# A decoder of four layers on one core: both expert mixtures sort all their tokens in one group

## The chip, the cores and the metric

The kernel runs on one core of a Trainium2 chip. Everything is float32. The time is the device time of one execution in microseconds; the comparison uses the median of several executions. TensorE does the matmuls and the transposes (a matmul with an identity), VectorE (DVE), ScalarE (ACT) and GpSimd (POOL) the elementwise work, SyncE (SP) starts the plain DMAs, and POOL also starts the indirect DMAs that scatter rows.

## The reference, cut to what matters

The activation x has 4 batches of 512 tokens of width 256. Twelve stages run one after the other, four layers of an attention, a cross attention and a feed-forward part:

```python
x = x + _L1_xattn_ref(ctx_1024, _layernorm(x), ...)      # the same form in layers 2 and 3
...
x = x + _L2_ffn_ref(_layernorm(x), router_w, w1, w2)
...
x = x + _L3_ffn_ref(_layernorm(x), Wg, W1, b1, W2, b2, W3, b3)
```

The cross attentions of layers 1 to 3 take their queries from the 512 tokens; keys and values come from the 512 tokens and from 64 rows of a second input, the context:

```python
kv = jnp.concatenate([x, lat], axis=1) @ Wkv
...
attn = jax.nn.softmax(dots, axis=-1)
out = jnp.einsum('bhij,bhjd->bhid', attn, v)
```

In the roles of the kernel, x of this excerpt is the 64-row context and lat the 512 tokens, so each head has 512 + 64 keys. The two feed-forward parts of layers 2 and 3 are mixtures of 8 experts, and each token goes to the two best:

```python
probs = jax.nn.sigmoid(xf @ router_w.T)                  # layer 2
topw, sel = jax.lax.top_k(probs, 2)                      # combine = topw / sum(topw)
h = jnp.square(jax.nn.relu(jnp.einsum('td,edw->tew', xf, W1e)))
out = jnp.einsum('ted,te->td', jnp.einsum('tew,ewd->ted', h, W2e), combine)
...
topv, topi = jax.lax.top_k(xt @ Wg.T, 2)                 # layer 3, weights softmax(topv)
h = jax.nn.silu(jnp.einsum('th,efh->etf', xt, W1) + b1) * (jnp.einsum('th,efh->etf', xt, W2) + b2)
eo = jnp.einsum('etf,ehf->eth', h, W3) + b3
```

## The kernel before

x stays in SBUF (`x_res`) as 16 token tiles of 128 tokens, four to a batch. Each stage is a function with one instruction list for each engine; between stages the engines meet. `sparse_experts` (from L4148) is run twice: turn 0 for layer 2, turn 1 for layer 3. It does not compute all experts for all tokens. It sorts rows by expert through HBM and multiplies only what is needed:

- **Routing.** DVE and ACT normalize the 16 tiles into `rows`, TensorE turns them in pieces of four (`piece_turned`, L4356) and multiplies with the router (`route`, L4367). DVE marks the two best experts of each token (`pick`: MAX8 at L4537, MATCH_REPLACE8 at L4540, the mask at L4543).
- **Places.** `rank` (L4376, L4378) counts with matmuls how many rows go to each expert ahead of each token, `put` (L4559 to L4584) makes from it the row index of each token's two copies, `weigh` (L4594 to L4609) the weights of the final sum.
- **Scatters.** POOL writes each token tile twice, once for each of its two experts, with indirect DMAs to `sorted_rows` in HBM (L4298). For the second copy the row's own number, its last column, is raised by one (L4336).
- **Tiles.** Since each expert's rows are rounded up to full tiles, n token tiles give (256 n + 8 x 127) / 128 sorted tiles, rounded down. The tokens are in two groups, `GROUP_TILES = (4, 12)`: 15 and 31, together 46 sorted tiles. SP loads them in chunks of 3 (`load_sorted`, L4264), after all scatters of their group. For each tile TensorE turns the rows (L4390), ACT copies the expert's up weights to a fixed place (L4494), TensorE multiplies up (L4404: 16 matmul records in turn 0, 32 in turn 1, where a second product is gated), ACT and DVE make the hidden rows, TensorE multiplies down (L4420), DVE copies the result to a ring of four buffers (L4678, in turn 1 with the bias at L4681), and POOL scatters it to its token's place in `expert_outputs` (L4307).
- **The second group inside the tiles.** Its `rank(1)`, `put(1)` and `weigh(1)` stand behind the second tile. Its 24 scatters stand in POOL's list between the output scatters: three, then one output, eight times over.
- **Final sums.** When the outputs are stored, SP fetches them (L4269), and DVE adds them to x with two operations per token tile, weight times row plus x (L4686, L4689). The first batch (4 token tiles) is fetched and added while later tiles run; 12 token tiles, 24 operations, stand at the end of the stage.

Before the first stage that needs them the weights are loaded by SP at the head of the stage: in turn 1 the columns of biases, 8 MB of up weights, 1 MB of bias rows (L4249) and 4 MB of down weights (L4250), all ahead of `load_sorted(0)`.

In the cross attentions of layers 1 to 3 the heads go in pairs, 8 pairs for each of four batches in layers 1 and 2, 4 in layer 3, 80 in all. For each pair `attended` (L2441, L2444) multiplies the values with the turned probabilities: for four key blocks of 128 and both heads (head h writes half h of the rows of a PSUM bank), then for the context block of 64 keys, where both weights and data of head h are on partitions 64h to 64h+63. The scores of the next pair (L2491) and the transposes of the probabilities (L2411) stand around it.

## Time and profile before

| | us |
|---|---|
| median of 3 executions | 3911.28 (3911.06 to 3914.19) |
| the profiled execution | 3942.55 |
| its span, first to last instruction | 3940.4 |
| l0 and l1_attn (0 to 605.65) | 605.65 |
| l1_xattn | 735.33 |
| l1_ffn and l2_attn | 608.82 |
| l2_xattn | 787.40 |
| l2_ffn, mixture, turn 0 (2737.2 to 2999.9) | 262.70 |
| l3_attn | 149.50 |
| l3_xattn | 444.10 |
| l3_ffn, mixture, turn 1 (3593.5 to 3940.4) | 346.90 |

TensorE is busy for 3495.3 us of the span (89%), VectorE for 2191.8 (56%), ScalarE for 1495.8 (38%) and GpSimd for 1370.0 (35%). In the l1_xattn stage TensorE is busy 701.45 of 735.33 us, in turn 0 of the mixture 212.15 of 262.70, in turn 1 285.71 of 346.90. The mean granted TensorE clock is 0.93 of full speed over the run, 0.85 over turn 0 and 0.89 over turn 1. A row of the timeline is one instruction or several of one kind in a row: its start, its length, the engine, the line, what it writes and reads, and in brackets how long the engine was idle before it and what released it.

### The profile page before, as it was taken

How to read it: one execution, taken by the hardware profiler on the slowest of the kernel's cores; microseconds unless marked ns; L12 is line 12 of the kernel's file. 1: busy time of each engine (PE TensorE's matmuls, PEld its weight loads, DVE VectorE, ACT ScalarE, POOL GpSimd, SP SyncE). 2: the span in 40 equal slices, each digit the busy share in tenths (PEclk: the TensorE clock that was granted, in tenths of full speed). 3: DMA queues.
4: the chain of work that ended last, by engine and by line, in shares of the span. 5: the costliest groups of instructions: out<-in, count | busy, mean ns of one | idle time of the engine just before them, and what ended most of it. 6: DMA issues, size and time to landing. Idle time of an engine off the chain costs nothing. (4 is left out here: it accounts for less than half of the span.)

```text
span 3940.4 us, 54458 instructions
## 1 busy us (share of the span) xinstructions
PE 3495.3 (89%) x18930; PEld 2240.6 (57%) x18930; DVE 2191.8 (56%) x5367; ACT 1495.8 (38%) x3040; POOL 1370.0 (35%) x1904
## 2 busy tenths in 40 slices
PE   7998897899999977888798999998896989995997
PEld 5675684445555566344444555555794445554896
DVE  5374444645556468666367676765234466664454
ACT  3253112433434364233244444443352144442453
POOL 2141441423323255232254444533422144442311
PEclk9999978999999988899799999999798889996998
DMA  2004001000000000000100000001221000003212
GB/s 100 1 1 123 14 1 46 1 1 1 1 1 1 13 1 24 1 1 1 49 1 1 1 1 1 1 1 76 99 80 57 4 25 1 1 1 160 71 60 84
DMA packets 48718, 108.85 MB, mean 28 GB/s; under 512 B 6660, under 2 KB 32900, under 8 KB 46404
## 3 DMA queue, kind: packets, MB, share of 16 engines
q1 hardware_dynamic: 40964, 84.88, 6.3%
q0 software_dynamic: 7488, 20.49, 1.5%
q8 instruction: 158, 2.59, 0.3%
q14 instruction: 108, 0.88, 0.1%
HBM read 70.67 MB, written 34.68 MB: 27 GB/s over the span
## 5 line engine op out<-in xcount | busy, mean ns | idle before, releaser
L2653 POOL TENSOR_SCALAR probs<-probs,inv_sum 128x512 f32<-128x512 f32 x640 | 437.7, 697 | 1008.3 <-DVE inv_sum L2774 1008.1
L2616 ACT ACTIVATE probs<-psum_banks,neg_max 128x576 f32<-128x576 f32 x640 | 468.5, 737 | 742.5 <-DVE neg_max L2857 742.5
L2857 DVE TENSOR_REDUCE neg_max<-psum_banks 128x1 f32<-128x576 f32 x640 | 455.0, 752 | 213.4 <-PE psum_banks L2491 206.8
L2491 PE MATMUL psum_banks<-keys_T,queries_T 64*128 64x288 f32 x2560 | 406.0, 436 | 52.5 <-ACT probs L2616 43.2
L2783 DVE COPY probs_T<-psum_banks 128x512 f32<-128x512 f32 x640 | 409.2, 681 | 4.5 <-PE psum_banks L2411 4.5
L2491 PEld LDWEIGHTS psum_banks<-keys_T,queries_T 64*128 64x128 f32 x2560 | 224.5, 189 | 269.2 <-ACT probs L2616 147.9
L2411 PE MATMUL psum_banks<-ident,probs 128*128 128x128 f32 x2560 | 356.5, 283 | 3.2 <-POOL probs L2653 2.3
L2411 PEld LDWEIGHTS psum_banks<-ident,probs 128*128 128x128 f32 x2560 | 280.3, 143 | 128.2 <-POOL probs L2653 63.3
L2441 PE MATMUL psum_banks<-probs_T,values 128*64 128x512 f32 x1280 | 310.9, 607 | 2.2 <-issue 2.2
L4404 PE MATMUL psum_banks<-sorted_T,tile_weights 128*128 128x128 f32 x2208 | 270.1, 279 | 9.2 <-ACT tile_weights L4494 4.9
L4404 PEld LDWEIGHTS psum_banks<-sorted_T,tile_weights 128*128 128x128 f32 x2208 | 262.2, 196 | 10.7 <-issue 10.6
L2853 DVE TENSOR_TENSOR psum_banks<-psum_banks,key_mask 128x128 f32<-128x128 f32 x192 | 57.5, 299 | 280.1 <-PE psum_banks L2491 280.1
L4420 PE MATMUL psum_banks<-w_L_experts_down,hidden_T 128*128 x736 | 183.3, 394 | 19.4 <-DVE expert_rows L4678 8.7
L4307 POOL DMA_INDIRECT expert_outputs<-expert_rows,output_index x92 | 90.3, 982 | 297.4 <-DVE expert_rows L4681 126.7
L2665 POOL TENSOR_TENSOR square_sum<-square_sum,neg_half 128x8 f32<-128x8 f32 x102 | 167.1, 1639 | 70.8 <-DVE square_sum L2749 69.3
L4420 PEld LDWEIGHTS psum_banks<-w_L_experts_down,hidden_T 128*128 128x128 f32 x736 | 137.4, 197 | 37.7 <-issue 21.7
L2346 PE MATMUL psum_banks<-w_L_xattn_Wkv,batch_normed_T 128*128 128x512 f32 x320 | 158.7, 620 | 0.0
L2441 PEld LDWEIGHTS psum_banks<-probs_T,values 128*64 128x64 f32 x1280 | 78.8, 136 | 133.8 <-issue 124.1
L4494 ACT COPY tile_weights<-w_L_experts_up 128x1024 f32 (+1 forms) x92 | 135.3, 1472 | 23.5 <-issue 23.5
L1962 ACT ACTIVATE probs_T<-psum_banks 128x512 f32<-128x512 f32 (+3 forms) x128 | 83.0, 701 | 127.7 <-PE psum_banks L1899 126.9
L2656 POOL TENSOR_TENSOR context_probs<-probs,inv_sum 128x128 f32<-128x128 f32 x320 | 128.9, 403 | 0.0
L2616 ACT ACTIVATION_READ_ACCUMULATOR probs<-psum_banks,neg_max 128x1 f32 x640 | 125.4, 196 | 0.0
(535 smaller groups left out, 6119.2 us busy)
## 6 DMA issues: line engine op xcount, KB each, us to landing
normed<-sorted_rows SPq DMA_DIRECT2D x30, 385.5 KB
sorted_rows<-zero_rows SPq DMA_DIRECT2D x8, 1028.0 KB, 14.5
w_L_experts_down<-in_L_experts_down SPq DMA_DIRECT2D x2, 4096.0 KB, 37.1
normed<-expert_outputs SPq DMA_DIRECT2D x8, 1024.0 KB, 7.9
w_L_xattn_Wkv<-in_L_xattn_Wkv SPq DMA_DIRECT2D x2, 2048.0 KB, 8.5
w_L_experts_up<-in_L_experts_up SPq DMA_DIRECT2D x1, 4096.0 KB, 13.0
sorted_rows<-zero_rows SPq DMA_DIRECT2D x4, 899.5 KB, 14.1
x_res<-in_x SPq DMA_DIRECT2D x4, 512.0 KB, 6.9
```

The source lines that it names most:

```text
L2346: last = pe.matmul(k.ps[:, 7, :], rows, wkv[:, c, W + a * 512:W + (a + 1) * 512], start=c == 0, stop=c == KC - 1)
L2411: last = pe.transpose(k.ps[:, 4 + n % 2, c * P:(c + 1) * P], prob[:, (b * NS + s) % PB, at + c * P:at + (c + 1) * P], k.ident[:, :])
L2441: last = pe.matmul(k.ps[r, 6, :], values[:, b % VB, c, (2 * j + h) * 64:(2 * j + h + 1) * 64], pT[:, q % 2, h, c, :], start=c == 0, stop=F ...
L2491: last = pe.matmul(k.ps[:, 2 * h + a, 0:HALF], qT[r, b % 2, j, t * P:(t + 1) * P], kT[r, j, k0:k0 + HALF], start=True, stop=True)
L2616: act.activation(prob[:, g % PB, h * w:(h + 1) * w].rearrange("p (a n) -> p a n", a=2), k.ps[:, 2 * h:2 * h + 2, 0:HALF], ACT.Exp, bias=nm ...
L2653: pool.tensor_scalar(w, w, inv[:, g % 4, h:h + 1], 1.0, ALU.mult, ALU.mult).then_inc(shared, 1)
L2665: pool.tensor_tensor(ss[:, i % 4, 2, :], ss[:, i % 4, 1, :], k.half[:, 0:8], ALU.pow).then_inc(inverted, 1)
L2783: dve.tensor_copy(pT[:, q % 2, h, :, t * P:(t + 1) * P], k.ps[:, 4 + n % 2, :].rearrange("p (c q) -> p c q", q=P)).then_inc(copied, 1)
L2857: dve.tensor_reduce(nmax[:, g % 4, h:h + 1], k.ps[:, 2 * h:2 * h + 2, 0:HALF], AX.XY, ALU.max, negate=True).then_inc(maxed, 1)
L4404: last = pe.matmul(ps[:, 2 * (n % 2) + part, f * P:(f + 1) * P], wt[:, n % 2, c, part * 512 + f * P:part * 512 + (f + 1) * P], xsT[:, n % ...
L4420: last = pe.matmul(ps[:, 6, 0:D], h[:, n % 2, f * P:(f + 1) * P], w_down[:, f // F, f % F * D:f % F * D + (E - 1) * STEP + D][:, bass.ds(a ...
L4494: act.copy(wt[:, n % 2, :, :], w_up[:, :, 0:(E - 1) * STEP + UP][:, :, bass.ds(at, UP)]).then_inc(weights_copied, 1)
```

## The change

- Each turn has its own groups, `MIXTURES = ((16,), (16,))`: one group of all 16 token tiles, which gives 39 sorted tiles. Routing, rank, places and weights are made once, for all tokens; all 32 scatters stand in POOL's list ahead of the first output scatter, and the first load of sorted rows waits for all of them. The ring of results has six buffers.
- ACT copies the up weights of the first two tiles before it moves the first turned rows.
- Final sums: all four batches are fetched at the end. For each token tile DVE adds the first row times its weight, ACT multiplies the second row by its weight in place, and POOL adds it to x.
- In turn 1 the bias rows and the down weights are loaded after the first two chunks of sorted rows; the columns of biases have a semaphore of their own.
- The context values of a pair get a block per head of 128 rows, in which the other head's 64 rows are zero (written once per stage by two DVE memsets); the context product then contracts over 128 rows.

```diff
-GROUP_TILES = (4, 12)
-GROUP_FIRST = (0, 4)
-GROUP_SORTED = tuple((2 * n * P + E * (P - 1)) // P for n in GROUP_TILES)
+MIXTURES = ((16,), (16,))
+HEAD = 4
...
-OUTPUT_RING = 4
+OUTPUT_RING = 6
...
-                sp.dma_start(w_down[:, :, :], w_down.src[:, :, :]).then_inc(down_loaded, 16)
+                if bias is None:
+                    load_late_weights()
...
                 load_sorted(0)
                 load_sorted(1)
+                if bias is not None:
+                    load_late_weights()
...
-                sp.wait_ge(combined, TT)
-                for b in range(1, B):
-                    fetch(b, TT * (b - 1))
+                for b in range(EARLY // TT, B):
+                    fetch(b, TT * b - EARLY)
...
+                if GROUPS == 1:
+                    pool.wait_ge(normed, NT)
+                    pool.wait_ge(indexed, 2)
+                    for t in range(NT):
+                        scatter(t, rows[:, t, :], 0, scattered_0)
+                    pool.wait_ge(copied_again, HEAD)
+                    for t in range(HEAD):
+                        scatter(t, again[:, t, :], 1, scattered_again)
+                    pool.wait_ge(scattered_0, first_scattered)
+                    late = rows[:, HEAD:NT, D:D + 1]
+                    pool.tensor_scalar(late, late, 1.0, 1.0, ALU.add, ALU.mult).then_inc(next_ids, 1)
+                    pool.wait_ge(next_ids, 1)
+                    for t in range(HEAD, NT):
+                        scatter(t, rows[:, t, :], 1, scattered_again)
...
                 for n in range(done, NTILES):
                     scatter_rows(n)
+                for t in range(EARLY, NT):
+                    pool.wait_ge(halfway, t + 1)
+                    pool.wait_ge(second_scaled, t - EARLY + 1)
+                    pool.tensor_tensor(k.x[:, t, :], k.x[:, t, :], got[:, t - EARLY, 1, :], ALU.add).then_inc(combined, 1)
...
+                for t in range(EARLY, NT):
+                    act.wait_ge(fetched[t // TT], 16)
+                    act.mul(got[:, t - EARLY, 1, :], got[:, t - EARLY, 1, :], gate[:, 1, t:t + 1]).then_inc(second_scaled, 1)
...
+                if GROUPS == 1:
+                    copy_weights(0)
+                    copy_weights(1)
 
                 move_rows(0)
                 move_rows(1)
-                copy_weights(0)
-                copy_weights(1)
...
-                                last = pe.matmul(k.ps[r, 6, :], vc[r, j, :], pTc[r, q % 2, :], start=False, stop=True)
+                                last = pe.matmul(k.ps[r, 6, :], vc[:, h, j, :], pTc[:, q % 2, :], start=False, stop=True)
```

POOL's list in turn 0, from the first scatter to the end of the stage, before. `sorted_rows_0` and `_1` are the two groups' sorted rows, `expert_outputs` the results:

```order
L4298 DMA sorted_rows_0<-normed,row_index 1920x257 x8
L4298 DMA sorted_rows_1<-normed,row_index 3968x257 x3
L4307 DMA expert_outputs<-expert_rows,output_index 9985x256
L4298 DMA sorted_rows_1<-normed,row_index 3968x257 x3
L4307 DMA expert_outputs<-expert_rows,output_index 9985x256
L4298 DMA sorted_rows_1<-normed,row_index 3968x257 x3
L4307 DMA expert_outputs<-expert_rows,output_index 9985x256
L4298 DMA sorted_rows_1<-normed,row_index 3968x257 x3
L4307 DMA expert_outputs<-expert_rows,output_index 9985x256
L4336 TENSOR_SCALAR normed<-normed 128x12
```

The same place after, to the end of the stage:

```order
L4324 DMA sorted_rows_0<-normed,row_index 4992x257 x20
L4355 TENSOR_SCALAR normed<-normed 128x12
L4324 DMA sorted_rows_0<-normed,row_index 4992x257 x12
L4333 DMA expert_outputs<-expert_rows,output_index 9089x256 x39
L4388 TENSOR_TENSOR x_res<-x_res,normed 128x256 x16
```

The 24 scatters that stood between output scatters now stand ahead of all of them, and 16 additions stand behind the last.

TensorE's list at the head of turn 0, before (pieces turned, routed, the first tiles, and the second group's rank behind them; the rank's matmuls shrink by 8 columns each, down to 128x8):

```order
L4367 MATMUL psum_banks<-w_L_ffn_router_w,normed 128x8 x16
L4390 MATMUL psum_banks<-ident,normed 128x128 x4
L4404 MATMUL psum_banks<-sorted_T,tile_weights 128x128 x8
L4390 MATMUL psum_banks<-ident,normed 128x128 x2
L4404 MATMUL psum_banks<-sorted_T,tile_weights 128x128 x8
L4376 MATMUL psum_banks<-gate_mask,w_before_token 128x104
L4378 MATMUL psum_banks<-gate_mask,ones 128x96
```

The same place after (here too the rank's matmuls shrink down to 128x8, and the tiles follow):

```order
L4411 MATMUL psum_banks<-w_L_ffn_router_w,normed 128x8 x16
L4420 MATMUL psum_banks<-gate_mask,w_before_token 128x136
L4422 MATMUL psum_banks<-gate_mask,ones 128x128
L4422 MATMUL psum_banks<-gate_mask,ones 128x120
```

The rank has moved from behind the second tile's product to ahead of the first turned tile, and covers 16 token tiles instead of 12.

SP's list at the head of turn 1, before:

```order
L4246 DMA w_L_bias_columns<-in_L_bias_columns 128x64
L4247 DMA w_L_experts_up<-in_L_experts_up 128x16384
L4249 DMA row_vectors<-in_rows 128x2048
L4250 DMA w_L_experts_down<-in_L_experts_down 128x8192
L4264 DMA normed<-sorted_rows_0 128x3x257 x5
```

And after:

```order
L4264 DMA w_L_bias_columns<-in_L_bias_columns 128x64
L4265 DMA w_L_experts_up<-in_L_experts_up 128x16384
L4287 DMA normed<-sorted_rows_0 128x3x257 x2
L4269 DMA row_vectors<-in_rows 128x2048
L4270 DMA w_L_experts_down<-in_L_experts_down 128x8192
```

Bias rows and down weights now stand behind the first two chunks of sorted rows.

## Rows read from the trace of the kernel before

**Rows 1.** TensorE's timeline, one pair in l1_xattn: start, length, then the instruction

```profile
773.46 1.03 PE L2441 MATMUL psum_banks<-probs_T,values 128*64 128x512 f32 x4
...
773.89 0.60 PE L2441 MATMUL psum_banks<-probs_T,values 128*64 128x512 f32 x2
...
774.42 1.08 PE L2444 MATMUL psum_banks<-context_probs_T,context_values 64*64 64x512 f32 x4
775.43 1.24 PE L2491 MATMUL psum_banks<-keys_T,queries_T 64*128 64x288 f32 x8
...
779.12 0.51 PE L2491 MATMUL psum_banks<-keys_T,queries_T 64*128 64x288 f32 x2 [1.42 <-ACT probs L2616]
```

**Rows 2.** Tile stretches: length, busy of PE, PEld, DVE, ACT, POOL, PEclk, DMA share, GB/s

```profile
2774.98:2971.72 196.74, 183.15 (x1186) 168.58 (x1187) 61.22 (x150) 89.14 (x134) 66.74 (x68) 0.93 0.24 78
3643.26:3906.11 262.85, 254.86 (x1906) 242.22 (x1907) 123.64 (x242) 130.94 (x135) 66.39 (x68) 0.99 0.18 59
```

**Rows 3.** Timeline of turn 0, last scatters, first tiles, second group's rank

```profile
2764.98 0.97 POOL L4298 DMA_INDIRECT sorted_rows<-normed,row_index  x1 [0.30 <-issue]
...
2767.80 11.75 SPq L4264 DMA_DIRECT2D normed<-sorted_rows  x3
...
2769.41 0.99 DVE L4537 MAX8 gate_top<-gate_row 128x8 f32<-128x14 f32 x12 [12.43 <-ACT gate_row L4473]
...
2771.04 0.66 PE L4390 MATMUL psum_banks<-ident,normed 128*128 128x128 f32 x2 [2.03 <-DMA normed<-sorted_rows]
...
2772.16 0.69 PE L4390 MATMUL psum_banks<-ident,normed 128*128 128x128 f32 x2 [0.46 <-ACT sorted_T L4482]
2772.26 0.21 DVE L4543 TENSOR_SCALAR gate_mask<-gate_marked 128x96 f32<-128x96 f32 x1
...
2774.98 3.75 PE L4404 MATMUL psum_banks<-sorted_T,tile_weights 128*128 128x128 f32 x16 [2.13 <-ACT tile_weights L4494]
...
2778.95 2.36 PE L4404 MATMUL psum_banks<-sorted_T,tile_weights 128*128 128x128 f32 x16
...
2781.35 2.76 PE L4378 MATMUL psum_banks<-gate_mask,ones 128*128 128x96 f32 x24
...
2787.64 0.97 POOL L4298 DMA_INDIRECT sorted_rows<-normed,row_index  x1 [21.69 <-DVE row_index L4574]
```

**Rows 4.** Timeline of turn 0, last tiles and final sums

```profile
2964.47 1.95 PE L4404 MATMUL psum_banks<-sorted_T,tile_weights 128*128 128x128 f32 x16
...
2968.21 1.95 PE L4404 MATMUL psum_banks<-sorted_T,tile_weights 128*128 128x128 f32 x16
...
2981.89 1.46 SPq L4269 DMA_DIRECT2D normed<-expert_outputs  x3
2987.44 0.48 DVE L4686 SCALAR_TENSOR_TENSOR x_res<-normed,gate_weights,x_res 128x256 f32<-128x256 f32 x1 [8.85 <-DMA normed<-expert_outputs]
...
2998.05 0.48 DVE L4689 SCALAR_TENSOR_TENSOR x_res<-normed,gate_weights,x_res 128x256 f32<-128x256 f32 x1
```

**Rows 5.** DVE and POOL beside each other in l3_attn (timeline)

```profile
3003.43 0.38 DVE L4064 TENSOR_SCALAR normed<-x_res,token_mv,token_rstd 128x256 f32<-128x256 f32 x1
...
3016.39 2.49 POOL L4039 TENSOR_TENSOR x_res<-x_res,row_vectors 128x512 f32<-128x512 f32 x2
...
3017.84 1.20 DVE L4064 TENSOR_SCALAR normed<-x_res,token_mv,token_rstd 128x256 f32<-128x256 f32 x1 [7.07 <-PE psum_banks L3913]
```

**Rows 6.** POOL's groups by form: an addition of 128x256 (busy, mean ns)

```profile
L2672 POOL TENSOR_TENSOR x_res<-x_res,row_vectors 128x256 f32<-128x256 f32 x32 | 22.3, 732 | 0.0
```

**Rows 7.** Timeline of turn 1, mask, first tile, two late tiles

```profile
3628.62 0.21 DVE L4543 TENSOR_SCALAR gate_mask<-gate_marked 128x96 f32<-128x96 f32 x1
...
3643.26 5.49 PE L4404 MATMUL psum_banks<-sorted_T,tile_weights 128*128 128x128 f32 x32 [2.76 <-ACT tile_weights L4494]
...
3889.77 3.74 PE L4404 MATMUL psum_banks<-sorted_T,tile_weights 128*128 128x128 f32 x32
3895.29 3.74 PE L4404 MATMUL psum_banks<-sorted_T,tile_weights 128*128 128x128 f32 x32
```

**Rows 8.** DMA issues of the page: count, KB each, us to landing

```profile
w_L_experts_up<-in_L_experts_up SPq DMA_DIRECT2D x1, 4096.0 KB, 13.0
```

220 lines of the change are left out of this document (127 added, 93 removed).

## The prediction

> **What bounds the kernel now.** I read the stages first, then the tile stretches of the two mixtures, then their two ends row by row. The reader is to see three things. In the mixtures the tiles bound, but not all of the time: turn 0 takes 196.74 us from the first tile's up product to the last one's, while two late tiles in a row start 3.73 us apart (2964.47, 2968.21), so 45 steps would be 167.9; 28.9 us are lost, TensorE is busy for only 183.15, and its clock is 0.93 [rows 2, 4]. Turn 1 takes 262.85 for 45 steps of 5.52 (3889.77 to 3895.29), 248.4; 14.4 are lost [rows 2, 7]. The loss stands where POOL's list holds three sorting scatters for each output scatter: 4 x 1.27 = 5.1 us of POOL (0.97 each and 0.30 of issue [rows 3]) against 3.73 for a tile, and four result buffers are soon full. Second, the head of each stage is a chain (mask, rank, places, scatters, load) in which TensorE mostly waits. Third, the cross attentions run on TensorE with little idle time; what the context product costs there counts 80 times.
>
> **Context product, 80 pairs.** It now has the form of its neighbours (contraction over 128 rows). The last two double steps of L2441: the one at 773.46 is followed by the next at 773.89, .43 for two records in one form; the last two before the form changes take 773.89 to 774.42, .53. The four context records take 774.42 to 775.43, 1.01; four of L2441, 773.46 to 774.42, take .96 although the form changes at their end [rows 1]. In one form, I expect .10 less at the change and .05 less in the product: 0.15 x 80 = **-12.0**. No row shows the new form in this place, so bounds: -8 (only the change, .10) to -13, and 0 as a rival. The next pair's scores find TensorE at once at 775.43, and the wait of 1.42 us at 779.12 is for ACT's probabilities, which follow from scores that also come earlier, so the saving carries on. The two memsets lie in DVE's wait for the context and cost nothing; if that cover were gone they would cost their own length once in a stage.
>
> The Trainium skill ("TensorEngine Tiling (Array Packing)", Theoretical Speedup) gives a product with a contraction of at most 64 rows up to twice the speed of the full array; by it a 128-row form would double the four records, +1.0 x 80 = +80. The rows speak against it: the 128-row records already run at .43 for two heads' halves, not slower than the 64-row ones at about .5. I give it no chance of its own beyond the rivals.
>
> **Turn 0, the head.** In the before case the mask of 12 token tiles ends at 2772.47. MAX8 to the mask took 2.85 for 12 tiles, so four more cost .95, and the fourth piece's routing in front of it some .3 (an estimate): 2773.7. The rank: 24 records took 2.76, .115 each; 16 token tiles need 34: 3.9 at the full clock. After an idle time TensorE runs at half (3.75 at 2774.98 for what later took 1.95 [rows 3, 4]), which gives 7.8. The clock comes back on the way; I take the middle, 6.0: 2779.8. From the rank's end (2784.11) to POOL's first scatter (2787.64) 3.53 passed; with 16 tiles 3.7: 2783.6. The 32 scatters go at 1.28, the ids raised in between cost about 1.0: the last starts 31 x 1.28 + 1.0 = 40.7 later, 2824.3. From the last scatter to the load 2.82 (2764.98 to 2767.80), to the first turned tile 3.24 (2771.04), to the up product 1.8: the second turning ends 1.12 + .69 behind the first's start, and the weights, which were copied late before (2.13 us of waiting at 2774.98), are there already. So the first up product starts at 2832.1, **+57.1** [rows 3].
>
> **Turn 0, the tiles.** No scatter stands between the outputs any more: POOL needs 1.27 a tile, six buffers. I take 3.73 throughout, and .6 for the first two tiles at a half clock (3.97 from 2774.98 to 2778.95, and part of the next) [rows 3, 4]. 39 tiles are 38 steps: 2832.1 + 141.7 + .6 = 2974.4 against 2971.72: **+2.7**. In terms: +57.1 head, -28.9 lost time, -26.1 for seven tiles, +.6. Bounds: the rank -2.1 to +1.8.
>
> **The final sums, each turn.** Before, the fetch is issued at 2981.89, DVE starts 5.55 later and ends at 2998.53: 16.64, of it 11.1 for 24 operations. Now 16 token tiles need .48 of DVE and .73 of POOL each [rows 4, 6], ACT's multiplication beside them. If DVE and POOL did not disturb each other, POOL would set the pace: 5.55 + .5 (the first DVE operation) + 16 x .75 = 18.0, +1.4. If one fully blocks the other, 1.21 each: 5.55 + 19.3 = 24.8, +8.2. The trace has such a meeting: POOL's two additions run 3016.39 to 3018.88, a DVE operation that alone takes .38 starts at 3017.84 and takes 1.20, to 3019.04 [rows 5]; had it waited for POOL's whole end it would have ended at 3019.26, so .22 overlapped. I take .48 + .73 - .22 = 1.0: 5.55 + .5 + 16.0 = 22.05, **+5.4** in each turn, +10.8 together.
>
> The Trainium skill ("SBUF — State Buffer", SBUF: two separate sides) says that a DVE operation with two SBUF inputs and a GpSimd operation that reads SBUF hold the shared port pair as an exclusive lock and the loser fully blocks. The trace agrees nearly. That is the upper bound, and a rival below.
>
> **Turn 1.** The mask ends at 3628.83. With the same +1.2 for 16 tiles and the same 58.4 from there to the up product (2773.7 to 2832.1), the first tile starts at 3688.5, +45.2 [rows 7]. 38 steps of 5.52 and .1: 3898.4 against 3906.11: -7.7. Then the late weights: the load is issued 5.0 before the first tile, 3683.5; 5 MB follow behind it. 4 MB took 13.0 to land [rows 8], so 5 MB take some 16.2, and they land at about 3700.5. The first down product is wanted behind the second up product: 3688.5 + 5.5 (half clock) + 3.9 = 3697.9. About 3 us of stall, and 1 for the clock that falls in it: +4.0 (bounds 0 to +6). Turn 1: **-3.7**. The waits added are `down_loaded` on TensorE, behind which only this tile's products stand, and `bias_loaded` on DVE at the first result, whose bias rows are issued before the down weights.
>
> **The sum.** -12.0 + 2.7 + 5.4 - 3.7 + 5.4 = -2.2. The profiled execution's span goes from 3940.4 to 3938.2, with the 2.15 around it 3940.4 instead of 3942.55. The profiled run stands 31.3 above the median; I take the difference as the same for both: 3911.28 - 2.2 = **3909.1**. Shorter loads of small arrays, ten instead of twelve fills and one sigmoid or exp less lie beside other work and count nothing.
>
> **Rivals.**
> - *The engines do not block each other in the sums.* For: the DVE result of tile t+1 does not touch what POOL adds for tile t, so the starts can interleave. Against: rows 5. Tails +1.4 each, sum -10.2: 3901.1; if the down weights are there in time too, -14.2: 3897.1.
> - *Full blocking*, as the page's rule would have it, 1.21 for each tile: tails +8.2 each, sum +3.4: 3914.7. For: rows 5, where .96 of 1.20 was a wait.
> - *Slower: the context product saves nothing*, since the .53 and 1.01 are not the form but the turn to other data, or since ACT's chain (softmax) bounds the pair. The point from which it decides is a pair whose scores wait for ACT, as at 779.12. Against: TensorE is 95% busy in that stage. Sum +9.8: 3921.1.
> - *Slower: the lost time in the tiles is not POOL's list*, but the loading of sorted rows beside the output scatters; then it stays with one group. Against: late in the turn, with loads and output scatters alike, steps are 3.73. +28.9 and +14.4 less half of what only the second group's start can explain (about 5): 3909.1 + 38 = 3947.
> - *The change does not do what it says*: the seven tiles less are fixed by the list, so no.
>
> **How the numbers follow.** Chances: forecast .48, no blocking .20, full blocking .14, nothing saved in the context .13, lost time stays .05. 0.2% is 7.8 us, about what a measurement tells from no change. Faster by more: .20, and .14 of the forecast's own spread (rank in time, context at -13, weights in time): .34. Slower by more: .13 + .05 and .05 of the spreads: .23. Within: .43. The range takes in all cases but the last: 3896 to 3922; the likeliest case's own is 3903 to 3915.
>
> **What would show it.** The context records: the four take .86 instead of 1.01, and the record before them follows at .43. The first up product of turn 0 lies about 95 us behind the stage's start instead of 37.8 (2774.98 - 2737.2), and steps are 3.73 from the third tile on. In the final sums POOL's additions start 1.0 apart (.7: the first rival; 1.2: the second). In turn 1 TensorE waits about 3 us for the DMA of the down weights ahead of the first down product. What would make it wrong: a step between tiles that isn't 3.73 and 5.52; scatters at a pace other than 1.28 when 32 stand in a row; a clock that comes back later than after the rank.

## The result and the profile after

The changed kernel takes 3957.47 us (median of four executions, 3955.79 to 3958.22), the kernel before in the same comparison 3912.74 (3911.06 to 3918.84): a ratio of 1.0108, with a 95% interval from 1.0096 to 1.012, 44.7 us slower. Three of the four executions of the kernel before are the ones of the table of before. The prediction was 3909.1 with a range that ended at 3922. It was wrong in sign and in size. One execution of the kernel before among the experiments (e12), of 12353.8 us at a granted clock of 0.45, is left out of its median.

A second number stands beside it from the start. The two traces differ by 13.7 us only (spans 3940.4 and 3954.1). The traced execution of the kernel before had taken 31 us more than its own median, that of the changed kernel takes what all its executions take. Where these 31 us belong is the larger part of what follows.

The stages of the changed kernel, from each stage's first load to the next one's: l1_xattn, l2_xattn, turn 0 of the mixture, l3_xattn, turn 1. The columns are those of [rows 2] (length, busy PE, PEld, DVE, ACT, POOL, clock, DMA share, GB/s):

```profile
608.87:1339.59 730.72, 696.66 (x3560) 389.28 (x3560) 395.32 (x762) 286.26 (x673) 228.18 (x395) 0.98 0.02 7
1949.64:2732.22 782.58, 737.40 (x3816) 414.71 (x3816) 509.83 (x1060) 346.26 (x774) 350.47 (x478) 0.97 0.02 7
2732.22:3009.35 277.13, 176.77 (x1144) 165.23 (x1144) 78.05 (x237) 98.26 (x159) 86.80 (x92) 0.77 0.28 99
3159.24:3599.30 440.06, 382.88 (x1928) 214.01 (x1928) 286.80 (x638) 178.34 (x394) 189.04 (x260) 0.95 0.02 7
3599.30:3954.10 354.80, 248.12 (x1768) 235.95 (x1768) 132.95 (x319) 133.06 (x159) 86.74 (x92) 0.81 0.27 98
```

Against the table of before: the cross attentions are 4.6, 4.8 and 4.0 us shorter, turn 0 is 14.4 longer, turn 1 7.9 longer. TensorE is busy for 177 of 277 us in turn 0, where it was busy for 212 of 263, and its mean clock there fell from 0.85 to 0.77: it has less to do and waits longer ahead of it. The first stage, whose code is the same, took 608.87 instead of 605.65.

The head of turn 0 after the change, against [rows 3]: the mask, the rank, the first and the last of 32 scatters, the first turned tile, and three up products:

```profile
2770.09 0.23 DVE L4598 TENSOR_SCALAR gate_mask<-gate_marked 128x128 f32<-128x128 f32 x1
...
2771.05 6.84 PE L4422 MATMUL psum_banks<-gate_mask,ones 128*128 128x128 f32 x32
...
2781.86 1.25 POOL L4324 DMA_INDIRECT sorted_rows<-normed,row_index  x1 [38.32 <-DVE row_index L4629]
...
2822.53 0.97 POOL L4324 DMA_INDIRECT sorted_rows<-normed,row_index  x1 [0.30 <-issue]
...
2828.75 0.66 PE L4434 MATMUL psum_banks<-ident,normed 128*128 128x128 f32 x2 [50.86 <-DMA normed<-sorted_rows]
...
2830.35 3.62 PE L4448 MATMUL psum_banks<-sorted_T,tile_weights 128*128 128x128 f32 x16
...
2834.19 1.95 PE L4448 MATMUL psum_banks<-sorted_T,tile_weights 128*128 128x128 f32 x16
...
2837.93 1.95 PE L4448 MATMUL psum_banks<-sorted_T,tile_weights 128*128 128x128 f32 x16
```

TensorE stands still for 50.86 us between the rank and the first turned tile. From there each tile follows the one ahead at 3.73 without a gap, which the tile stretches of both turns show, first to last up product:

```profile
2830.35:2972.14 141.79, 141.79 (x980) 132.38 (x980) 44.38 (x98) 75.30 (x113) 34.97 (x36) 0.99 0.21 65
3697.62:3913.76 216.14, 211.33 (x1587) 201.31 (x1587) 96.93 (x174) 109.62 (x114) 34.98 (x36) 0.98 0.19 65
```

In turn 0 TensorE is busy for all of 141.79 us. In turn 1 4.8 us are idle, in one place, the wait for the down weights that the prediction has:

```profile
3697.62 5.43 PE L4448 MATMUL psum_banks<-sorted_T,tile_weights 128*128 128x128 f32 x32
...
3703.10 3.74 PE L4448 MATMUL psum_banks<-sorted_T,tile_weights 128*128 128x128 f32 x32
3711.66 3.54 PE L4464 MATMUL psum_banks<-w_L_experts_down,hidden_T 128*128 x8 [4.81 <-DMA w_L_experts_down<-in_L_experts_down]
```

And the end of turn 0, against [rows 4]: the fetch, the first operations of DVE and POOL (16 of each in a row), and the next stage's first operation on DVE:

```profile
2982.43 2.28 SPq L4292 DMA_DIRECT2D normed<-expert_outputs  x4
...
2987.97 12.99 DVE L4749 SCALAR_TENSOR_TENSOR x_res<-normed,gate_weights,x_res 128x256 f32<-128x256 f32 x16 [8.92 <-DMA normed<-expert_outputs]
2988.63 13.60 POOL L4388 TENSOR_TENSOR x_res<-x_res,normed 128x256 f32<-128x256 f32 x16 [7.77 <-ACT normed L4567]
...
3009.40 1.47 DVE L4057 BATCH_NORM_STATS2 token_stat<-x_res 128x6 f32<-128x256 f32 x4 [8.43 <-PEq L45]
```

The additions run at 0.85 us a token tile and end at 3002.23, 19.80 us behind the fetch. Then 7.2 us pass in which no engine computes. Before, the next stage began 1.5 us behind DVE's last operation (2998.53 in [rows 4] to 2999.99).

### The profile page after: what moved, and what is told of

Its sections match the earlier page's. It is cut to its first block and busy times, and to the rows that moved or that the text cites. A ratio compares the mean times of both kernels' runs of the same rounds, so it can differ in the third digit from the quotient of the medians.

```text
span 3954.1 us, 53033 instructions
## 1 busy us (share of the span) xinstructions
PE 3414.8 (86%) x18450; PEld 2187.3 (55%) x18450; DVE 2155.6 (55%) x5225; ACT 1475.0 (37%) x3028; POOL 1379.2 (35%) x1922
## 5 line engine op out<-in xcount | busy, mean ns | idle before, releaser
L4448 PE MATMUL psum_banks<-sorted_T,tile_weights 128*128 128x128 f32 x1872 | 225.1, 278 | 0.0
L4448 PEld LDWEIGHTS psum_banks<-sorted_T,tile_weights 128*128 128x128 f32 x1872 | 218.9, 195 | 0.1
L4333 POOL DMA_INDIRECT expert_outputs<-expert_rows,output_index x78 | 75.8, 972 | 317.0 <-DVE expert_rows L4744 142.7
L4464 PE MATMUL psum_banks<-w_L_experts_down,hidden_T 128*128 x624 | 149.4, 383 | 7.0 <-DMA w_L_experts_down<-in_L_experts_down 4.8
L4532 ACT COPY tile_weights<-w_L_experts_up 128x1024 f32 (+1 forms) x78 | 114.6, 1472 | 46.6 <-DVE weight_offsets L4639 28.1
L4464 PEld LDWEIGHTS psum_banks<-w_L_experts_down,hidden_T 128*128 128x128 f32 x624 | 113.7, 192 | 20.5 <-issue 8.0
```

The lines of the kernel that those rows point to most:

```text
L4448: last = pe.matmul(ps[:, 2 * (n % 2) + part, f * P:(f + 1) * P], wt[:, n % 2, c, part * 512 + f * P:part * 512 + (f + 1) * P], xsT[:, n % ...
L4464: last = pe.matmul(ps[:, 6, 0:D], h[:, n % 2, f * P:(f + 1) * P], w_down[:, f // F, f % F * D:f % F * D + (E - 1) * STEP + D][:, bass.ds(a ...
```

## The experiments

All ratios are to the kernel before, run beside it on the same chip. There were six sessions, each on another chip: on four of them the kernel before takes 3941 to 3944 us, on two 3912. The executions of a session agree in this. No chip was used in two sessions, so chip and session can't be told apart; "kind of chip" below means no more than that. On which chips the comparison above and the first trace were taken is not known.

| kernel | before there | this, us | ratio (95% interval) |
|---|---|---|---|
| e0 before | 3942.7 | 3941.3 | 1.0000 (0.9986 to 1.0014) |
| e1 before + context product | 3942.7 | 3932.3 | 0.9974 (0.9965 to 0.9984) |
| e2 change, two groups in both turns | 3942.7 | 3922.5 | 0.9946 (0.9929 to 0.9963) |
| e3 change, sums on DVE | 3942.7 | 3944.3 | 1.0009 (0.9999 to 1.0019) |
| e4 change | 3941.8 | 3955.6 | 1.0035 (1.0024 to 1.0045) |
| e5 change, early weights | 3941.8 | 3948.5 | 1.0011 (1.0001 to 1.0020) |
| e6 change, one group in turn 0 only | 3941.8 | 3935.6 | 0.9981 (0.9971 to 0.9991) |
| e7 change, one group in turn 1 only | 3941.8 | 3936.7 | 0.9986 (0.9974 to 0.9997) |
| e8 two groups, sums on DVE | 3943.9 | 3907.8 | 0.9907 (0.9892 to 0.9922) |
| e9 one group, sums on DVE, early weights | 3943.9 | 3937.9 | 0.9985 (0.9976 to 0.9994) |
| e10 change, last six tiles' sums on DVE | 3943.9 | 3944.5 | 1.0003 (0.9994 to 1.0012) |
| e11 as e8, four result buffers | 3912.5 | 3885.1 | 0.9932 (0.9919 to 0.9946) |
| e12 before / e13 change | 3941.4 | 3937.4 / 3954.9 | 0.9991 / 1.0036 (1.0021 to 1.0051) |
| e14 before / e15 change | 3911.7 | 3915.8 / 3952.0 | one execution each |

### Is it 44.7 us or 13.9: the two kernels run again

No edit in any of these.

> The kernel before, unchanged. Its profiled execution took 3942.55 us, 31 more than the median of its plain ones (3911.28), while the changed kernel's profiled and plain executions agree (3955.79 against 3957.47). Theory A: the kernel before has two ways to run, and the trace that was read is of the longer one; a fresh trace is then near 3912 and shows which stretch is 31 us shorter, by my reading the lost time in the tile stretches (28.9 us in turn 0, 14.4 in turn 1). Theory B: the profiler itself costs it 31 us, and the fresh trace is at 3942 again with plain executions at 3912. Theory C: the difference lies in other stages, and the tile stretches lose 28.9 and 14.4 us in both.

> The changed kernel, unchanged, once more beside the kernel before on the same chip. The comparison on record gave a ratio of 1.0108 (44.7 us), but the two traces differ by 13.7 us of span only, and on the chip of the first experiments the kernel before takes 3942.7 us instead of 3912.7. Theory A: the 31 us are the chip's or the session's, not the change's, and side by side the ratio is what the traces say: 13.7 us, 1.0035 (3956 where before is 3943). Theory B: the changed kernel costs 45 us wherever it runs; then 3988 where before is 3943. Theory C: the changed kernel is at 3950 to 3957 on every chip, and only the kernel before moves between 3912 and 3943; the ratio then depends on the chip, 1.002 to 1.011.

The kernel before took 3941.3 there, so theory B of the first, that the profiler costs the 31 us, falls: plain and traced executions agree on that chip. The changed kernel took 3955.6 beside 3941.8, 13.9 us or 0.35% more, as the two traces had said (13.7). But 3955.6 is also within 2 us of what it had taken in the comparison on record (3957.5), where the kernel before was at 3912.7. Only one of the two kernels moves with the chip, theory C of the second. To see where, a trace of the kernel before on the faster kind of chip was needed.

> The kernel before, once more. On three chips it took 3942 to 3944 us, on a fourth 3912.5, as in its first executions. The kernel with two groups, DVE sums and four buffers, traced on that fourth chip, had a tile stretch of turn 0 (first to last up product) of 175.6 us, against 192.8 for its sister with six buffers traced on another. Theory: if this execution falls on a chip where the time is 3912, its tile stretches take some 178 and 253 us instead of 193 to 198 and 263; where it is 3942, they are as before. Rival: the stretches are the same in both, and the 31 us lie in other stages.

> The changed kernel once more, on the same chip as the run above. Theory: its tile stretches run at 3.73 and 5.52 us a tile whatever the chip, so it takes 3954 to 3958 on every chip; the ratio is 1.0035 where the kernel before takes 3942 and 1.011 where it takes 3912. Rival: it moves with the chip as the kernel before does, and the ratio stays 1.0035.

This pair fell on a chip of the slower kind and repeated the numbers: 3937.4 and 3954.9. The next pair fell on the faster kind.

> The kernel before, a third time, in search of a chip where it takes 3912 us. Theory: on such a chip its two tile stretches take some 178 and 253 us instead of 193 to 198 and 263, all other stages as before. Rival: the stretches are the same, and the 31 us lie in other stages. On a chip where it takes 3942 the run tells only that the stretches are at 193 to 198 and 263 again.

> The changed kernel beside it: 3950 to 3958 on either kind of chip by the theory, 3925 on the faster kind by the rival.

The kernel before took 3915.8 (and 3911.7 in the execution beside it), the changed one 3952.0, one execution each. The tile stretches of the kernel before on this chip, first to last up product of each turn, and turn 0 and turn 1 as a whole, the counterparts of [rows 2]:

```profile
2779.80:2955.61 175.81, 173.15 (x1186) 161.37 (x1187) 61.35 (x150) 89.39 (x134) 65.86 (x68) 0.98 0.27 87
3623.89:3879.75 255.86, 253.63 (x1910) 241.91 (x1910) 124.06 (x242) 131.01 (x135) 68.14 (x68) 0.99 0.19 60
...
2742.15:2983.60 241.45, 202.12 (x1328) 187.12 (x1328) 91.66 (x302) 105.12 (x165) 80.53 (x83) 0.88 0.35 121
3573.40:3913.50 340.10, 286.02 (x2064) 270.92 (x2064) 156.75 (x402) 146.33 (x165) 82.66 (x83) 0.88 0.30 108
```

The stretches take 175.81 and 255.86 instead of 196.74 and 262.85: 20.9 and 7.0 us less, together 27.9, where the two spans (3940.4 and 3913.5) differ by 26.9; the other stages differ by 5 us at most, up and down. With 45 steps of 3.73 and 5.52, only 7.9 and 7.5 us are lost there. So the time that the change was to win back, 28.9 and 14.4 us in [rows 2], is mostly not there on this kind of chip. In turn 0 all of the 7.9 stand in the first three steps from tile to tile (4.0, 7.1 and 8.1 us, up product to up product, instead of 3.73), where the second group's rank runs on TensorE and DVE works out its places; the trace of [rows 3] has the same three (4.0, 7.0 and 8.6). What differs between the chips comes behind them.

What the lost time looks like where it is lost. The kernel before in its first trace, TensorE's timeline:

```profile
2821.02 1.95 PE L4404 MATMUL psum_banks<-sorted_T,tile_weights 128*128 128x128 f32 x16
2828.36 3.78 PE L4420 MATMUL psum_banks<-w_L_experts_down,hidden_T 128*128 x8 [5.38 <-issue]
2831.93 0.63 PE L4390 MATMUL psum_banks<-ident,normed 128*128 128x128 f32 x2
2832.35 3.67 PE L4404 MATMUL psum_banks<-sorted_T,tile_weights 128*128 128x128 f32 x16
2837.52 3.51 PE L4420 MATMUL psum_banks<-w_L_experts_down,hidden_T 128*128 x8 [1.50 <-DVE expert_rows L4678]
```

The same list on the faster kind of chip, at the same place of the program, with the same 24 scatters and 8 outputs in POOL's list and the same four buffers:

```profile
2802.73 1.95 PE L4404 MATMUL psum_banks<-sorted_T,tile_weights 128*128 128x128 f32 x16
...
2806.47 1.95 PE L4404 MATMUL psum_banks<-sorted_T,tile_weights 128*128 128x128 f32 x16
...
2810.20 1.95 PE L4404 MATMUL psum_banks<-sorted_T,tile_weights 128*128 128x128 f32 x16
...
2813.93 1.95 PE L4404 MATMUL psum_banks<-sorted_T,tile_weights 128*128 128x128 f32 x16
```

Steps of 3.73 while POOL scatters at 1.28. No result waits for a buffer in either of the two traces: DVE's copies into the ring (`expert_rows`) never wait for a stored output. And the waits of the first trace in its first 75 us of tiles (engine, what waited, for what: us, times, longest) name releasers that are no program step:

```profile
ACT hidden_T L4509 <- remote: 11.5, 2, 6.7
...
DVE hidden_T L4650 <- issue: 10.1, 2, 7.1
...
PE psum_banks L4420 <- issue: 5.4, 1, 5.4
```

With "remote" and "issue" the profile names no instruction of the program that ended the wait. In the same stretch on the faster chip no operation of DVE and no matmul waits for either. Over the whole traces, waits of this kind of 3 us or more on TensorE, ACT or DVE are in no trace from the faster kind (e11, e14, e15) and in no trace of the changed kernel (after, e4, e13, e15). In the traces of two groups from the slower kind there are 2 to 14, up to 10.9 us long, all but at most one of each trace where the second group's scatters run between tiles; that one, 3.7 to 3.9 us of ACT in turn 0, lies beside the first group's scatters. e6 has them in turn 1 only and e7 in turn 0 only, each in its turn of two groups. What holds the engines there on some chips no view of the trace names. That stays open.

### The context product alone

```diff
-                                last = pe.matmul(k.ps[r, 6, :], vc[r, j, :], pTc[r, q % 2, :], start=False, stop=True)
+                                last = pe.matmul(k.ps[r, 6, :], vc[:, h, j, :], pTc[:, q % 2, :], start=False, stop=True)
```

(e1: with the two-block `vc` and its memsets, on the kernel before)

> The kernel before with the context product of the changed kernel alone. The trace after shows the three cross attention stages shorter by 4.6, 4.8 and 4.0 us, 13.4 together, and the stages ahead of them longer by 3.2. Theory: -13 us against the kernel before, 3899 in plain executions (ratio 0.9966). Rival: what the context product gives is eaten in the stages ahead, since the 3.2 us belong to it: -10. A second rival: the plain executions differ from the profiled ones in these stages and nothing is gained.

It gave 10.5 us, between theory and rival, and the interval (0.9965 to 0.9984, 6 to 14 us) decides for neither. The traces are sharper. The eight value records and the ones behind them, before, with [rows 1], and after:

```profile
772.55 1.94 PE L2441 MATMUL psum_banks<-probs_T,values 128*64 128x512 f32 x8
...
775.08 1.94 PE L2443 MATMUL psum_banks<-probs_T,values 128*64 128x512 f32 x8
776.84 1.03 PE L2446 MATMUL psum_banks<-context_probs_T,context_values 128*64 128x512 f32 x4
777.80 1.24 PE L2493 MATMUL psum_banks<-keys_T,queries_T 64*128 64x288 f32 x8
```

The four context records take 0.96 (776.84 to 777.80) where they took 1.01, and follow the start of the eight value records after 1.76 (1.77 as the median) where it was 1.87 (772.55 to 774.42). That is 0.05 in the product and 0.10 at the change of form, in the median of the pairs of every stage, 0.15 x 80 = 12 us. The three stages are together shorter by 12 to 17 us in all traces with this form, against the first trace of the kernel before, and by 8 to 12 against e14.

### One group or two

```diff
-MIXTURES = ((16,), (16,))
+MIXTURES = ((4, 12), (4, 12))      # e2; ((16,), (4, 12)) in e6, ((4, 12), (16,)) in e7
```

> The changed kernel with the two groups of 4 and 12 token tiles in both turns again; the final sums on three engines for the last 12 token tiles, six result buffers, the late weights of turn 1 and the context product stay. If the one group is what costs the 44.7 us, this one is at the time before less the context product: 3900 to 3908, the three-engine sums and late weights adding 3 to 8 us. If the late weights and sums cost most of it, it stays near 3940. By the profiled stages alone (turn 0 +14.4, turn 1 +7.9) the whole mixture part would be only 22 us, and two groups would be at 3935.

> The changed kernel with one group in turn 0 and two groups (4 and 12 token tiles) in turn 1. Turn 0 took 277.1 us with one group (trace after) and 262.7 with two (the kernel with two groups in both turns). Theory: 14 us slower than the kernel with two groups in both turns (3922.5), 3937. Rival: what one group costs sits in turn 1, and this kernel is at 3925.

> The changed kernel with two groups in turn 0 and one group in turn 1. Turn 1 took 354.8 us with one group (trace after) and 338.6 with two groups and the same late weights. Theory: 16 us slower than the kernel with two groups in both turns, 3938.5, and the two single-group turns add up to the changed kernel, 3952. Rival: the sum is not the parts, since the first turn's length moves the second's clock: more than 5 us off.

With two groups the changed kernel would have been 20 us faster than before on the slower kind of chip. Its two groups are not quite those of before: the second group's rank stands behind the first tile, not the second. One group in turn 0 costs 13 us of that, in turn 1 14, both 33 (ratios 0.9946, 0.9981, 0.9986, 1.0035, over two chips of the slower kind). e2's own expectation had reckoned 22 us for both; the stages of its trace are 14.4 and 16.2 us shorter than those of the changed kernel. That the two costs add up to 27 and not 33 is the rival of e7, but the intervals (4 us and more to either side of each) do not separate 27 from 33. All this is where two groups still lose 25 us in the tiles of turn 0; no kernel with one group in one turn was run on the faster kind.

### The final sums

```diff
                 for t in range(EARLY, NT):
-                    pool.wait_ge(halfway, t + 1)
-                    pool.wait_ge(second_scaled, t - EARLY + 1)
-                    pool.tensor_tensor(k.x[:, t, :], k.x[:, t, :], got[:, t - EARLY, 1, :], ALU.add).then_inc(combined, 1)
...
-                    if t >= EARLY:
-                        return
```

(e3: ACT's loop removed as well, so that DVE makes both operations of each token tile)

> The changed kernel with the final sums on DVE alone (32 operations at 0.46 us, 14.8 us, behind the fetch of all four batches), nothing on ACT and POOL. In the trace after, 7.1 us pass from POOL's last addition (3002.23) to the next stage's start (3009.35), 1.4 us passed from DVE's last before. Theory: the 5.7 us are POOL's own way out of the stage, which was hidden while POOL had been idle for 20 us; then this kernel has a gap of 1.4 and turn 0 is 5 us shorter, turn 1 0.5 longer: 3953 in all. Rival: the gap belongs to the new stage layout and stays: 3958.

3944.3 against 3955.6 for the change, on two chips of the slower kind: 11 us less (ratios 1.0009 and 1.0035) with all 32 operations on one engine, where the theory had some 5. In its trace turn 0 is 5.1 us shorter than in the changed kernel's, as expected, and turn 1 2.2 shorter, not 0.5 longer. The gap is gone (DVE's last operation, the next stage's first):

```profile
2994.98 0.48 DVE L4745 SCALAR_TENSOR_TENSOR x_res<-normed,gate_weights,x_res 128x256 f32<-128x256 f32 x1
...
2996.99 0.76 DVE L4057 BATCH_NORM_STATS2 token_stat<-x_res 128x6 f32<-128x256 f32 x2 [1.53 <-PEq L45]
```

To see whether the gap is POOL's, the last six token tiles were given to DVE:

```diff
-                for t in range(EARLY, NT):
+                for t in range(EARLY, NT - 6):
                     pool.wait_ge(halfway, t + 1)
...
+                    if t == NT - 6:
+                        dve.wait_ge(combined, NT - 6)
```

> The changed kernel with the last 6 of 16 token tiles summed on DVE alone (two operations each), the first 10 on three engines; GpSimd is done some 5 us before the stage ends. Theory A: the 7.1 us from the last addition to the next stage in turn 0 are GpSimd's branch out of the stage and its four clears of semaphores, run after its last addition; then the gap falls to about 1.5 us, and the tail from fetch to next stage from 26.9 to 5.5 + 10 x 0.85 + 12 x 0.46 + 1.5 = 21.5. Theory B: the gap comes with ACT or with the new stage layout; it stays at 7 us. In time: A is 8 us faster than the changed kernel (3948, ratio 1.0015), B the same or 1 us slower.

```profile
2994.04 8.60 POOL L4388 TENSOR_TENSOR x_res<-x_res,normed 128x256 f32<-128x256 f32 x10 [7.80 <-ACT normed L4567]
...
3007.26 0.48 DVE L4756 SCALAR_TENSOR_TENSOR x_res<-normed,gate_weights,x_res 128x256 f32<-128x256 f32 x1
...
3009.81 1.41 DVE L4057 BATCH_NORM_STATS2 token_stat<-x_res 128x6 f32<-128x256 f32 x4 [2.06 <-PEq L45]
```

POOL ends at 3002.64, DVE at 3007.74, and the next stage starts at 3009.81: 7.17 us behind POOL and 2.07 behind DVE. In the changed kernel it was 7.17 behind POOL too (3002.23 to 3009.40). With DVE alone it is 1.5 behind DVE, so in e10 the stage still waits for POOL, by half a microsecond. The gap is POOL's, as theory A says, but not for the clears of semaphores that the theory names. POOL's sequencer has a DRAIN at the end of the stage; here are the kernel before and the changed one (count, the shortest, median and longest of the two turns in ns, the first and the last start):

```profile
L4227 POOLq DRAIN  x2: 7627/7631/7635, 2979.2 to 3917.0; - x2
...
L4244 POOLq DRAIN  x2: 7092/7097/7102, 3001.0 to 3945.7; - x2
```

In the changed kernel it runs from 3001.01 to 3008.11, 5.88 us past the last addition; the clears and the meeting of the engines take the other 1.3, and they are in the 1.5 us of before too. In the kernel before the DRAIN was over at 2986.84, while DVE was still at its sums. Its length is nearly the same with a scatter as POOL's last work (e3, 7.07) as with an addition (7.10); what sets it no run shows. In time e10 is 11 us faster than e4 by the medians of two chips (ratios 1.0003 and 1.0035, some 5 us of uncertainty), and 7.3 by the two turns of the traces; 8 was forecast.

### The late weights

```diff
-                if bias is None:
-                    load_late_weights()
+                load_late_weights()
...
-                if bias is not None:
-                    load_late_weights()
```

> The changed kernel with bias rows and down weights of turn 1 loaded at the head of the stage again, as before the change. In the trace after, TensorE waits 4.8 us for the down weights at 3706.8 and its first down product takes 3.54 at the halved clock instead of 1.89: 6.5 us. Theory: this kernel is 6.5 us faster than the changed one beside it. Rival: the 5 MB at the head slow the stores of sorted rows, and half of it is lost: 0 to 3 us.

7.1 us less, and turn 1 is 6.5 shorter in the trace. The second up product and the first down product of turn 1 follow one another at the full clock:

```profile
3699.56 3.74 PE L4445 MATMUL psum_banks<-sorted_T,tile_weights 128*128 128x128 f32 x32
3703.13 1.89 PE L4461 MATMUL psum_banks<-w_L_experts_down,hidden_T 128*128 x8
```

### What is left of the one group, and a version that is faster

e9 joins the edits of e3 and e5. e8 is e3 with two groups in both turns; its late weights stay. The second group's rank stands behind the first tile here too.

> The changed kernel with both repairs: final sums on DVE alone and bias rows and down weights loaded at the head of turn 1. Alone they gave 11.3 us and 7.1 us. What is left of the change is the one group and the context product. Theory: the two add up, 3955.6 - 18.4 = 3937, ratio 0.9988, so that the one group alone costs some 6 us against two groups in the form of before (3932.3 with the context product). Rival: they overlap (the shorter tail moves nothing when the clock falls again), 3944, ratio 1.0005.

> Two groups in both turns, the context product, six result buffers and late weights of turn 1 kept, the final sums on DVE alone (24 operations for the last 12 token tiles). With two groups and the three-engine sums the time was 3922.5 (0.9946 of before); its stages took 23.8 us from the fetch to the next stage in turn 0 and 24.2 to the end in turn 1, against 18.0 and 20.7 before. Theory: the two sums give back 5.8 + 3.5 us: 3913, ratio 0.9923. Rival: with late weights and more result buffers the DVE sums meet the fetch of the last batch and give nothing: 3922.

The repairs add up: 3937.9, as worked out. The one group, repaired and with the gain of the context product in it, is 6 us faster than before on the slower kind of chip. On the faster kind it was not run; from e9's 17.7 us under e4 and the 44.7 of the comparison it would be some 27 us slower than before, an estimate. The two-group version is 36 us faster than before on the slower kind, 5 us better than its theory. In turn 1 the late weights, which cost 7 us with one group, gain time with two: the last of the first eight scatters is issued 27.5 us behind the stage's start in both kernels, but the first chunks of sorted rows are issued 31.5 us behind it instead of 41.9, where the 5 MB stood ahead of them and the down weights landed at 41.2. The first up product starts 37.7 us behind the stage's start instead of 49.8. No run has two groups with early weights on the changed kernel, so this is read from the traces:

```profile
3606.17 0.91 SPq L4287 DMA_DIRECT2D normed<-sorted_rows  x2
3607.13 0.48 SPq L4269 DMA_DIRECT2D row_vectors<-in_rows  x1
```

The whole turn takes 331.80 instead of 346.9 (the columns of [rows 2] again):

```profile
3574.70:3906.50 331.80, 283.63 (x2064) 266.99 (x2064) 156.40 (x402) 145.90 (x165) 81.28 (x83) 0.91 0.31 111
```

Against e8, e11 changes the ring of results alone, `OUTPUT_RING = 4`:

> The two-group kernel with DVE sums (3907.8, ratio 0.9907) with four result buffers instead of six, nothing else. From the first to the last up product of turn 0 it took 192.8 us for 45 steps of 3.73 (167.9), so 25 us are lost with six buffers too; the kernel before loses 28.9. Theory: the buffers are not what stalls, since POOL's list of 24 scatters among 8 outputs runs at its own 1.28 us and two more buffers only shift the wait: same time within 3 us, ratio 0.9907 to 0.9915. Rival: the buffers give 3 to 6 us in each turn, and this kernel is at 3914 to 3920 (0.9925 to 0.994).

It fell on a chip of the faster kind (before at 3912.5), where it is 27 us faster than before. So its ratio, 0.9932, says nothing of the buffers against 0.9907. Its own trace does. In it the tiles run at 3.73 from the second on, and then DVE waits for stored outputs, four times in a row, of which these are the first three:

```profile
2809.81 0.42 DVE L4732 COPY expert_rows<-psum_banks 128x256 f32<-128x256 f32 x1 [1.19 <-DMA expert_outputs<-expert_rows,output_index]
...
2814.91 0.42 DVE L4732 COPY expert_rows<-psum_banks 128x256 f32<-128x256 f32 x1 [2.55 <-DMA expert_outputs<-expert_rows,output_index]
...
2819.99 0.42 DVE L4732 COPY expert_rows<-psum_banks 128x256 f32<-128x256 f32 x1 [3.83 <-DMA expert_outputs<-expert_rows,output_index]
```

They are 5.1 us apart, the pace of POOL's list, and three steps of TensorE take 4.84, 5.08 and 5.74 us instead of 3.73: 4.5 us more, of which 0.4 are a wait for sorted rows and the rest is lost to a ring of four, as the rival said of this turn and the theory did not. In turn 1 nothing waits for a stored output. Six buffers on this kind of chip were not run. The trace, in which turn 0 took 239.4 us, was also the first sign that the rest of the lost time goes with the chip.

## Why the prediction was wrong, point by point

**The context product: right.** -12.0 predicted, -13.4 in the trace after, -10.5 timed alone. The mechanism (one form, no change) and the size hold, 0.10 and 0.05 us a pair. The sign that the prediction gives for it, .86 for the four context records, is not what its own working says (1.01 less .05), and they took 0.96.

**The head of turn 0: right in kind, 3 us short.** The first up product was to start 94.9 us behind the stage's start and started at 98.1. The scores were ready 1.6 later than taken, and the rank took 7.42 (2770.47 to 2777.89), nearly the upper bound of 7.8, not the middle of 6.0: TensorE ran at half its clock (granted 0.50) through all 34 records. Scatters (1.28), load and turning came as in [rows 3].

**The lost time: the step that failed.** The sum took -28.9 and, inside turn 1's -7.7, -14.4 from [rows 2], times of one traced execution, and set them against a median 31.3 us lower with the sentence that the difference is the same for both kernels. It was not: the 31 us and the lost time are largely the same microseconds. In the one trace of the kernel before from a chip where it takes 3912 (e14) only 7.9 and 7.5 us are lost. Put into the sum of the prediction, this makes +27.9, and -2.2 becomes +25.7.

The mechanism was wrong as well. The prediction says that POOL's list (5.1 us for an output against 3.73 for a tile) fills four buffers. Its own rows leave the ring just short of full: eight outputs at 5.1 us are 41 us, in which TensorE makes 11 tiles, three more than are stored, and the ring holds four. In the kernel before no result waits for a buffer on either kind of chip, and e14 has the same list, four buffers and steps of 3.73. The mechanism exists, but is small: in e11, where the results are further ahead of their scatters from the start, it costs some 4 us. Of the 28.9 us of turn 0 some 8 belong to the first three steps, with the second group's rank, on both kinds of chip, and the rest to pauses whose cause is open. The rival that the lost time is not POOL's list was given .05; it expected the time to stay with one group, but with one group it did go, on every chip. What no rival said is that it might hardly be there in the executions that are compared.

**The final sums: +10.8 predicted, some +15 in the traces.** The pace is 0.85 us a token tile (13.60 for 16), below the 1.0 taken and well below the 1.21 of full blocking, so the sums themselves cost 3.2 us more than before in turn 0, not 5.4. The Trainium skill ("SBUF — State Buffer", SBUF: two separate sides) gives full blocking for this pair of operations; the trace does not agree, at 0.85 where the two alone take 0.48 + 0.73. DVE's operations do grow, 12.99 for 16 or 0.81 each, from 0.46. The 1.0 came from a meeting of another operation, a TENSOR_SCALAR of DVE [rows 5]; and of its 1.20 us .82 was the wait (1.20 less the .38 that it takes alone), not .96. What was left out is POOL's way out of the stage, its DRAIN: 5.7 us in turn 0, and about 2 of the 6.0 us by which turn 1 is longer behind its fetch (26.7 against 20.7; 24.5 in e3, where DVE makes all sums). The prediction asked what hides each added step, but not what had been hidden behind POOL's idle time. A term for it is in neither the sum nor a rival.

**The late weights: right place, 6.5 instead of 4.0.** TensorE waited 4.81 for the down weights and the first down product took 3.54 instead of 1.89; early weights gave 7.1 back in e5. The upper bound was 6. In turn 0, where nothing was moved, nothing changed.

**The sum.** With the measured sizes, on the slower kind of chip: -13.4 context, +5.4 in turn 0 up to the last up product, +1.9 in turn 1, +8.9 and +6.0 behind the two fetches (with small changes between), +3 in the first stage, whose code did not change: the 13.7 us of the traces. On the faster kind the lost time of before is 27.9 less, and the two single executions there differ by 36.2, the medians on record by 44.7. Of the 8.5 us between these two numbers 5.8 could be the first stage, which took 610.6 us in that execution of the kernel before and 604.9 in that of the changed one; that it is the same in the medians no trace shows, and the rest is not assigned. On the slower kind, where the lost time is won back in full, the forecast of -2.2 is wrong too: against +13.7 it lacks some 3 us at the head of each turn, 2.5 in the late weights and 4 in the sums, and the 4.8 by which the first stage and two others, unchanged in code, came out longer, less the 1.4 that the context product gave beyond its term.

## What to carry to other kernels

When the traced execution and the median differ by more than the effect that is predicted, find the stage that holds the difference before a gain is read from that trace; lost time in which engines wait for nothing that the profile names is a candidate to vanish in the executions that count. Before a full queue is named as a cause, compare its backlog with the depth of the ring behind it, and look whether anything waits for a free buffer. And when the last step of a stage goes to an engine that had been idle, its own way out of the stage (here 7.2 us on GpSimd, most of it a DRAIN) comes out from under the others.

## What the runs showed of the hardware

- The same kernel takes 3941 to 3944 us on four chips and 3912 on two, in one session each; the difference sits where indirect DMAs of one group run beside the tiles of another (175.8 against 193 to 198 us for turn 0's tiles). A kernel without that overlap takes 3952 to 3957 beside either time.
- From GpSimd's last addition to the next stage's start pass 7.17 us with one group and 7.74 with two (e2, e7), of which the DRAIN of its sequencer runs on for 5.9 and more; from DVE's last operation, with GpSimd long done, 1.46 to 1.53. The DRAIN takes 7.1 to 7.7 us in the mixture stages whether GpSimd's last work was a scatter or an addition.
- An addition on GpSimd and a multiply-add on DVE, both from SBUF, run beside each other at 0.85 us a pair where they take 0.73 and 0.46 to 0.48 alone: neither free nor one after the other. ACT's multiplications ran beside them.
- After 4.45 us of idle time TensorE ran 34 records of the rank at a granted clock of 0.50 (1.2 GHz), 0.22 us each instead of 0.115. In the changed kernel its mean granted clock over turn 0 is 0.77 of full speed, where it was 0.85: the same records take longer in a kernel that makes TensorE wait more, and eat part of what fewer records save.
- The first stage, with the same instructions, took 604.4 to 611.4 us in the traces; the clock granted from 150 to 300 us was 0.93 or 0.94 where it took 609 to 611, and 0.97 or 0.98 where it took 604 to 608.
